# Two attention blocks in one kernel: the first transfers on the sync queue in another order

## The chip, the cores and the metric

The kernel runs on one core of a Trainium2 chip. The metric is the device time of one execution in microseconds (us), as the median of several runs. The core has a matrix engine (TensorE, PE in the rows), a vector engine (VectorE, DVE), an activation engine (ScalarE, ACT), GpSimd (POOL) and a sync engine (SyncE, SP) that in this kernel issues all the transfers. The transfers run on 16 DMA engines behind one queue.

## The reference

The input is `x` and a context, each 64 batches of 128 tokens of width 256 in float32. Block 0 is cross-attention with 16 heads of 64 and an MLP, block 1 is windowed cross-attention with one shared key and value head, a gate and a norm. Cut to what matters:

```python
def block0(q, c):                       # k and v are both the context c
    qn, kn, vn = ln(q, gq, bq), ln(c, gk, bk), ln(c, gv, bv)
    s = einsum(qn Wq, kn Wk) + rel_bias[i - j]
    o = softmax(s / 8) @ (vn Wv) @ fc_w.T + fc_b
    x = q + o
    return x + gelu(ln(x) @ W1.T + b1) @ W2.T + b2

def block1(q, c):                       # one key and value head of 16, window of +-64
    s = where(window, (q Wq + bq)(c Wk + bk) / 4, -1e9)
    a = softmax(s) @ (c Wv + bv) @ Wo + bo
    g = silu([a, q] @ Wg + bg)
    y = a * g + q * (1 - g)
    y = y * rsqrt(mean(y * y) + 1e-6) * rms_w
    return y - mean(y over tokens)
```

## The kernel before

Two batches make a group, and 32 groups are worked through in a software pipeline. Each engine has its own program, a list written out by hand; programs meet only at semaphores (`till.wait_ge(name, count)`), and an engine that waits holds back everything behind it in its list. Float32 weights are split into a high part (ScalarE, `weight_hi_scaled`) and a rest (VectorE, `weight_lo_scaled`), so that a product is three matmuls of a faster type. The gain of the layer norm is multiplied into the weight at that moment, and the shift goes through the weights once, as a matmul (`bias_mm`, one for each half of a weight).

The change lies in the prologue, where the weights, the constants and the data of group 0 come in. The list of transfers stands in `sync_program` (L440 to L457 and on). Weights pass through five staging buffers (`SOFT0`, `SOFTT0`, `HID`, `SOFTT1`, `SOFT1`): half of the query weights goes to SOFT0 and half to SOFTT0, half of the key weights to HID and half to SOFTT1, the first half of the value weights to SOFT1. The second half of the value weights comes later, once more into SOFT0.

Group 0 needs the mean and the reciprocal deviation of each token laid out along the free axis. VectorE takes them from the token-major tiles (`tokens` for x, `first_tokens` for the context; L1477, L1500, L1525, L1533), GpSimd takes the power (L3013, L3021), VectorE transposes (`flip_x` L1543, `flip_c` L1551), and the sync queue writes the result to DRAM (`out_x` L327, `out_c` L354) and reads it back spread over all 128 partitions (`in_x` L331, `in_c` L369). `in_x` waits until what `out_x` wrote has landed, `in_c` the same for `out_c`. The feature-major tiles (`raw_x` L315, `raw_c` L321) are then normalised: x on GpSimd (`x_less` L3051, `x_norm` L3057), the context on VectorE (`first_c_less` L1560, `first_c_norm` L1566). ScalarE makes the high part of x in `x_hi` (L2466).

VectorE's list begins: statistics of x, statistics of the context, `scale_bq1` (L1442, waits for `cols`), `var_c`, `flip_x`. So the flip of x stands behind the context's tokens.
ScalarE's list begins: high parts of the query weights (twice), the key weights (twice), the first half of the value weights, then `x_hi`, `c_hi`, and the second half of the value weights.
TensorE's list begins, in this order:

```python
bias_mm(banks[0], SOFT0, 1, shifts[0], 0)
bias_mm(banks[0], SOFTT0, 1, shifts[0], 1)
bias_mm(banks[2], HID, 1, shifts[1], 0)
bias_mm(banks[2], SOFTT1, 1, shifts[1], 1)
kv(0, banks[0], ("bias", 1))
bias_mm(banks[2], SOFT1, 1, shifts[2], 0, ("bias", 2))
proj_q(0, 0, banks[7])
bias_mm(banks[2], SOFT0, 2, shifts[2], 1)
proj_k(0, 0, banks[1])
```

`cols` holds the gains, shifts and biases that are read by partition (14.5 KB). `relb` holds the relative bias (64 KB), `rows` the constants that are read along the free axis, the same on every partition (648 KB of writes), and `wkv1` the key and value weights of block 1 (32 KB). The last three share the semaphore `consts_in`, which counts to 48. `rows` is first read by `bias_plus` (L1434) and by `kv_out`.

Of the kernel before, what the change touches and what calls it, by code (L numbers as in the profile page):

```python
# [12 lines left out]
P = 128  # L13
# [15 lines left out]

ONCE = ("filled", "ident_made", "masked", "scaled", "bias_mm", "bias_turned", "bias", "w_hi", "w_lo", "bv_hi", "bcol", "fold", "wo_wg",  # L30
        "cols_in", "consts_in", "raw0", "raw1", "raw2", "raw3", "raw4", "x_in", "tokens_in", "raw_in", "stat_out", "stat_in", "stored",
        "keys_out", "keys_in", "spread0", "spread1_0", "spread1_1", "first_tokens", "first_raw", "first_out", "first_in")


def two_block_xattn(nc, t):
# [25 lines left out]
    with ExitStack() as ctx:  # L61
# [27 lines left out]
        rows = sb("rows", [P, 5 * D + HD])  # L89
# [84 lines left out]
        def by_chunk(ap):  # L174
            return ap.rearrange("(k p) n -> p k n", p=P)
# [85 lines left out]
        def sync_program(sp):  # L261
# [115 lines left out]

            def consts_in():
                sp.dma_start(relb[:], t["rel"]).then_inc(sem["consts_in"], 16)
                sp.dma_start(rows[:], t["rows"].partition_broadcast(P)).then_inc(sem["consts_in"], 16)  # L380
                sp.dma_start(wkv1[:], by_chunk(t["wkv1"])).then_inc(sem["consts_in"], 16)

            def q1_gx_in():
                till.wait_ge("w_lo", 11)
# [48 lines left out]
            def store(g, b):  # L433
# [3 lines left out]
                till.wait_ge("y_out", n + 1)  # L437
                sp.dma_start(t["out"][n], gate_of(g, b)).then_inc(sem["stored"], 16)

            tokens_c(0)  # L440
            tokens_x(0)
            weight_in(SOFT0, t["wq_t"][0:P, :])
            cols_in()
            weight_in(SOFTT0, t["wq_t"][P:2 * P, :])
            weight_in(HID, t["wk_t"][0:P, :])
            weight_in(SOFTT1, t["wk_t"][P:2 * P, :])
            consts_in()
            out_x(0)
            raw_x(0)
            out_c(0)  # L450
            weight_in(SOFT1, t["wv_t"][0:P, :])
            raw_c(0)
            in_x(0)
            in_c(0)
            weight_in(HID, half_of(t["fc_t"], 1), ("w_lo", 3), ("bias_mm", 3))
            weight_in(SOFT0, t["wv_t"][P:2 * P, :], ("w_lo", 1), ("bias_mm", 1))
            weight_in(SOFTT0, half_of(t["fc_t"], 0), ("w_lo", 2), ("bias_mm", 2))  # L457
# [149 lines left out]
        def tensor_program(pe):  # L607
# [69 lines left out]
            def kv(g, bank, *drains):  # L677
                if not there(g):
                    return
                if g == 0:  # L680
                    till.wait_ge("consts_in", 48)
                freed(till, *drains)
                src = first_raw if g == 0 else raw[:]
                if g == 0:
                    till.wait_ge("first_raw", 16)
                else:
                    till.wait_ge("raw_in", loads(g, 2))
                for k in range(KD):
                    of_block = src[:, k, :].rearrange("p (b j a) -> p j b a", b=GROUP, j=NB)
                    for j in range(NB):  # L690
                        last = pe.matmul(bank[j * BLOCK:(j + 1) * BLOCK, 0:GROUP * BLOCK], wkv1[:, k, :],
                                         of_block[:, j, :, :], start=(k == 0), stop=(k == KD - 1), skip_group_check=True)
                last.then_inc(sem["kv"], 1)
# [720 lines left out]
        def vector_program(dve):  # L1414
# [15 lines left out]
            def bias_plus(dst, src, stage_of, count):  # L1430
                till.wait_ge(stage_of, count)
                till.wait_ge("cols_in", 16)
                till.wait_ge("consts_in", 48)
                dve.tensor_tensor(dst, src, dst, ALU.add).then_inc(sem["bias"], 1)  # L1434

            def bias_b1(bank):
# [5 lines left out]
                dve.tensor_scalar(bq1[:], bq1[:], -SCALE1, None, ALU.mult).then_inc(sem["scaled"], 1)  # L1442

            def scale_rel():
                till.wait_ge("consts_in", 48)
                dve.tensor_scalar(relb[:], relb[:], -SCALE0, None, ALU.mult).then_inc(sem["scaled"], 1)

            def spread_bv():
# [139 lines left out]
            def kv_out(g):  # L1588
                if not there(g):
                    return  # L1590
                if g == 0:
                    till.wait_ge("consts_in", 48)
                    till.wait_ge("filled", 1)
                till.wait_ge("kv_turn", g + 1)
                if g >= NK1:
# [1915 lines left out]
```

## Time and profile before

| | us |
|---|---|
| median of 3 runs | 1853.11 |
| lowest, highest | 1852.79, 1853.65 |
| the profiled execution's own time | 1853.23 |
| its span in the trace | 1851.4 |
| PE busy in the span | 1798.8 (97%) |
| DVE busy | 1485.9 (80%) |
| ACT busy | 1543.2 (83%) |
| POOL busy | 1294.0 (70%) |

The span is what the trace covers; 1.8 us of the execution lie around it. A row of the time line gives the start, the duration, the engine and line, the operation with the tile it writes and reads, and in brackets how long the engine had been idle and what released it. The row of a transfer on SPq shows only its issue; the time until it has landed is in the view of the DMAs. PE's ends are modelled, so the distance between two starts says more than the duration of one matmul.

### The profile page before, as it was taken

How to read it: one execution, taken by the hardware profiler on the slowest of the kernel's cores; microseconds unless marked ns; L12 is line 12 of the kernel's file. 1: busy time of each engine (PE TensorE's matmuls, PEld its weight loads, DVE VectorE, ACT ScalarE, POOL GpSimd, SP SyncE). 2: the span in 40 equal slices, each digit the busy share in tenths (PEclk: the TensorE clock that was granted, in tenths of full speed). 3: DMA queues.
4: the chain of work that ended last, by engine and by line, in shares of the span. 5: the costliest groups of instructions: out<-in, count | busy, mean ns of one | idle time of the engine just before them, and what ended most of it. 6: DMA issues, size and time to landing. Idle time of an engine off the chain costs nothing.

```text
span 1851.4 us, 54940 instructions
## 1 busy us (share of the span) xinstructions
PE 1798.8 (97%) x18532; PEld 1664.1 (90%) x18532; DVE 1485.9 (80%) x6755; ACT 1543.2 (83%) x5586; POOL 1294.0 (70%) x1324
## 2 busy tenths in 40 slices
PE   6999999999999999999999999999999999999984
PEld 4989999999999999999999999999999999999973
DVE  6878788887788887788887788887888887878764
ACT  4788888888888888888888888888888888888874
POOL 3656777766777766777766777776777776777654
PEclk9999999999999999999999999999999999999997
DMA  7434445444445444444444444444444444444432
GB/s 234 122 97 112 127 116 129 119 110 111 128 117 129 119 112 111 123 121 125 119 114 112 120 125 122 119 119 108 121 123 124 116 119 114 117 116 118 102 87 57
DMA packets 238057, 219.07 MB, mean 118 GB/s; under 512 B 48848, under 2 KB 220240, under 8 KB 237776
## 3 DMA queue, kind: packets, MB, share of 16 engines
q1 hardware_dynamic: 237776, 215.57, 45.4%
q8 instruction: 147, 2.41, 0.5%
q14 instruction: 134, 1.10, 0.2%
HBM read 71.29 MB, written 9.96 MB: 44 GB/s over the span
## 4 chain that ended last, share of the span: by engine, by line
PE 94%; DVE 2%; DMA 1%; POOL 1%; issue 1%; ACT 1%; SPq 0%; POOLq 0%; DVEq 0%
PE bank L611 12%; PE bank L613 11%; PE bank L612 11%; PE bank L625 9%; PE bank L629 8%; PE bank L626 8%; PE bank L779 7%; PE bank L792 7%; PE bank L904 4%; PE bank L917 4%; PE bank L617 3%; PE bank L618 3%; PE bank L621 3%; PE bank L635 2%; DVE soft L1739 1%
## 5 line engine op out<-in xcount | busy, mean ns | idle before, releaser
L2585 ACT ACTIVATE soft<-soft,row_min 128x128 f32<-128x128 f32 x1024 | 397.3, 392 | 65.9 <-DVE row_min L1739 65.8
L2505 ACT ACTIVATE soft<-soft,row_min 128x128 f32<-128x128 f32 x1024 | 398.5, 393 | 17.0 <-DVE row_min L1631 13.1
L3034 POOL TENSOR_TENSOR soft<-soft,inv_sum 128x512 f32<-128x512 f32 x256 | 271.9, 1062 | 169.7 <-DVE inv_sum L1639 169.6
L234 DVE STREAM_TRANSPOSE turned<-soft 128x512 f32<-128x512 f32 x512 | 342.1, 689 | 10.4 <-POOL soft L3034 4.8
L3043 POOL TENSOR_TENSOR soft<-soft,inv_sum 128x512 f32<-128x512 f32 x256 | 264.6, 1045 | 63.5 <-DVE inv_sum L1748 63.4
L1739 DVE CUSTOM_DVE_ANT_0 soft<-bank,winb 128x128 f32<-128x128 f32 x1024 | 230.5, 284 | 44.3 <-PE bank L904 37.2
L1631 DVE CUSTOM_DVE_ANT_0 soft<-bank,relb 128x128 f32<-128x128 f32 x1024 | 230.4, 284 | 22.7 <-PE bank L779 14.0
L2505 ACT ACTIVATION_READ_ACCUMULATOR soft<-soft,row_min 128x1 f32 x1024 | 194.8, 190 | 0.0
L2585 ACT ACTIVATION_READ_ACCUMULATOR soft<-soft,row_min 128x1 f32 x1024 | 194.2, 190 | 0.0
L779 PE MATMUL bank<-kT,qT 64*128 64x128 f32 x2048 | 148.7, 284 | 3.5 <-DVE kT L1611 0.5
L779 PEld LDWEIGHTS bank<-kT,qT 64*128 64x128 f32 x2048 | 125.0, 187 | 26.0 <-issue 20.8
L611 PE MATMUL bank<-wv,cT 128*128 128x256 f32 x512 | 147.6, 288 | 0.0
L613 PE MATMUL bank<-wv,cT 128*128 128x256 f32 x512 | 144.8, 283 | 0.0
L612 PE MATMUL bank<-wv,cT 128*128 128x256 f32 x512 | 144.8, 283 | 0.0
L792 PE MATMUL bank<-soft,V 128*64 128x128 f32 x2048 | 140.1, 279 | 0.7 <-DMA soft<-turned 0.4
L1702 DVE TENSOR_TENSOR hidS<-hid,hidS 128x1024 fp32r<-128x1024 f32 x64 | 84.9, 1326 | 64.4 <-ACT hidS L2556 62.7
L792 PEld LDWEIGHTS bank<-soft,V 128*64 128x64 f32 x2048 | 109.2, 136 | 29.6 <-issue 19.6
L1611 DVE TENSOR_SCALAR kT<-bank,bk 128x256 f32<-128x256 f32 x256 | 110.2, 472 | 29.8 <-PE bank L779 28.2
L625 PE MATMUL bank<-wfc,OT 128*128 128x256 f32 x512 | 133.7, 294 | 0.0
L2487 ACT ACTIVATE qT<-bank,bq 128x256 f32<-128x256 f32 x256 | 106.9, 470 | 31.2 <-PE bank L779 25.5
L626 PE MATMUL bank<-wfc,OT 128*128 128x256 f32 x512 | 127.5, 282 | 0.0
L625 PE MATMUL bank<-w,hidS 128*128 128x256 f32 x512 | 126.9, 281 | 0.0
(247 smaller groups left out, 6495.4 us busy)
## 6 DMA issues: line engine op xcount, KB each, us to landing
soft<-turned SPq DMA_DIRECT2D x1024, 128.0 KB, 2.7
tokens<-stats_by_row SPq DMA_DIRECT2D x63, 256.0 KB, 3.6
tokens<-in_x SPq DMA_DIRECT2D x32, 256.0 KB, 2.7
raw<-in_x_t SPq DMA_DIRECT2D x32, 256.0 KB, 3.3
x<-in_x SPq DMA_DIRECT2D x32, 256.0 KB, 2.7
out<-gate SPq DMA_DIRECT2D x63, 128.0 KB, 2.6
tokens<-in_ctx SPq DMA_DIRECT2D x31, 256.0 KB, 2.8
raw<-in_ctx_t SPq DMA_DIRECT2D x31, 256.0 KB, 2.7
```

The source lines that it names most:

```text
L234: return eng.transpose(turned[:, slot, :, s % 2, :, :].rearrange("p j h b -> p h j b"), soft[:, s, :, :].rearrange("p h (j a) -> p h j a", ...
L611: pe.matmul(out, stat(LO), mov(HI), start=first, stop=False, **kw)
L612: pe.matmul(out, stat(HI), mov(LO), start=False, stop=False, **kw)
L613: return pe.matmul(out, stat(HI), mov(HI), start=False, stop=last, **kw)
L625: pe.matmul(out, stat(HI), mov(LO), start=first, stop=False, skip_group_check=True)
L626: return pe.matmul(out, stat(HI), mov(HI), start=False, stop=False, skip_group_check=True)
L779: last = pe.matmul(bank[i][:, h * SEQ:(h + 1) * SEQ], qT[half, c, b * SEQ:(b + 1) * SEQ], kT[half, c, b * SEQ:(b + 1) * SEQ], start=True, ...
L792: last = pe.matmul(bank[row:row + HS, col:col + SEQ], V[:, b, c * P + row:c * P + row + HS], pair_of_slots(Q % 2)[:, :, slot, h, :], start ...
L2505: last = act.activation(soft[:, s, h, :], soft[:, s, h, :], ACT.Exp, bias=row_min[:, s, h:h + 1], scale=-1.0, accum_out=row_sum[:, s, h:h ...
L2585: last = act.activation(soft[:, s, h, :], soft[:, s, h, :], ACT.Exp, bias=row_min[:, s, h:h + 1], scale=-1.0, accum_out=row_sum[:, s, h:h ...
L3034: pool.tensor_tensor(soft[:, m % NS0, :, :], soft[:, m % NS0, :, :], inv_sum[:, m % NS0, :].unsqueeze(2).broadcast_to([P, QUAD, SEQ]), ALU ...
L3043: pool.tensor_tensor(soft[:, s, :, :], soft[:, s, :, :], inv_sum[:, s, :].unsqueeze(2).broadcast_to([P, QUAD, SEQ]), ALU.mult).then_inc(se ...
```

## The change

The transfers at the head of the sync queue are put in another order. The tokens of x are issued first and the context's tokens fourth; `cols` is issued second instead of fourth. `out_x`, `raw_x` and `in_x` come ahead of the second half of the key weights (`SOFTT1`). Behind that half come `out_c`, the constants, `raw_c` and `in_c`, then the first half of the value weights. The constants lose `rows`, which gets a transfer of its own behind the value weights, and a semaphore of its own (`rows_in`). The waits that counted to 48 now count to 32, or wait for `rows_in` where `rows` is read. The lists of the other engines keep their order.

```diff
             def consts_in():
                 sp.dma_start(relb[:], t["rel"]).then_inc(sem["consts_in"], 16)
-                sp.dma_start(rows[:], t["rows"].partition_broadcast(P)).then_inc(sem["consts_in"], 16)
                 sp.dma_start(wkv1[:], by_chunk(t["wkv1"])).then_inc(sem["consts_in"], 16)
+
+            def rows_of_all():
+                sp.dma_start(rows[:], t["rows"].partition_broadcast(P)).then_inc(sem["rows_in"], 16)
...
+            tokens_x(0)
+            cols_in()
+            weight_in(SOFT0, t["wq_t"][0:P, :])
             tokens_c(0)
-            tokens_x(0)
-            weight_in(SOFT0, t["wq_t"][0:P, :])
-            cols_in()
             weight_in(SOFTT0, t["wq_t"][P:2 * P, :])
             weight_in(HID, t["wk_t"][0:P, :])
-            weight_in(SOFTT1, t["wk_t"][P:2 * P, :])
-            consts_in()
             out_x(0)
             raw_x(0)
+            in_x(0)
+            weight_in(SOFTT1, t["wk_t"][P:2 * P, :])
             out_c(0)
+            consts_in()
+            raw_c(0)
+            in_c(0)
             weight_in(SOFT1, t["wv_t"][0:P, :])
-            raw_c(0)
-            in_x(0)
-            in_c(0)
+            rows_of_all()
             weight_in(HID, half_of(t["fc_t"], 1), ("w_lo", 3), ("bias_mm", 3))
             weight_in(SOFT0, t["wv_t"][P:2 * P, :], ("w_lo", 1), ("bias_mm", 1))
...
                 if g == 0:
-                    till.wait_ge("consts_in", 48)
+                    till.wait_ge("consts_in", 32)
...
             def bias_plus(dst, src, stage_of, count):
...
-                till.wait_ge("consts_in", 48)
+                till.wait_ge("rows_in", 16)
...
             def scale_rel():
-                till.wait_ge("consts_in", 48)
+                till.wait_ge("consts_in", 32)
...
                 if g == 0:
-                    till.wait_ge("consts_in", 48)
+                    till.wait_ge("rows_in", 16)
                     till.wait_ge("filled", 1)
```

## Rows read from the trace of the kernel before

**Rows 1.** The page, part 1: busy time and share of the span.

```profile
PE 1798.8 (97%) x18532; PEld 1664.1 (90%) x18532; DVE 1485.9 (80%) x6755; ACT 1543.2 (83%) x5586; POOL 1294.0 (70%) x1324
```

**Rows 2.** Time line of PE (start, duration, engine, operation, idle before).

```profile
9.41 1.08 PE L645 MATMUL bank<-hid,cols 128*32 128x256 f32 x8
10.71 1.08 PE L645 MATMUL bank<-soft,cols 128*32 128x256 f32 x8 [0.23 <-DMA soft<-in_wk_t]
...
16.78 1.11 PE L645 MATMUL bank<-soft,cols 128*32 128x256 f32 x8
22.13 0.55 PE L617 MATMUL bank<-xT,wq 128*128 128x256 f32 x1 [4.24 <-ACT xT L2466]
...
24.11 1.08 PE L645 MATMUL bank<-soft,cols 128*32 128x256 f32 x8
...
25.50 0.42 PE L618 MATMUL bank<-cT,wk 128*128 128x256 f32 x1
25.72 0.41 PE L617 MATMUL bank<-cT,wk 128*128 128x256 f32 x1
...
27.66 0.28 PE L611 MATMUL bank<-cT,wk 128*128 128x256 f32 x1
27.78 0.28 PE L612 MATMUL bank<-cT,wk 128*128 128x256 f32 x1
```

**Rows 3.** Time line of the sync queue: start and length of an issue.

```profile
0.72 0.45 SPq L301 DMA_DIRECT2D x<-in_ctx  x1
...
7.25 0.69 SPq L327 DMA_DIRECT2D stats_by_row<-stat_rows  x1
...
12.54 0.33 SPq L331 DMA_DIRECT2D tokens<-stats_by_row  x1
13.48 0.32 SPq L369 DMA_DIRECT2D x<-stats_by_row  x1
...
14.33 0.50 SPq L268 DMA_DIRECT2D soft<-in_wv_t  x1
...
33.91 0.52 SPq L327 DMA_DIRECT2D stats_by_row<-stat_rows  x1
35.96 0.33 SPq L331 DMA_DIRECT2D tokens<-stats_by_row  x1
```

**Rows 4.** View of the DMAs, issues at 14.33 and 35.96: KB, us to landing.

```profile
soft<-in_wv_t SPq DMA_DIRECT2D x1, 512.0 KB, 9.4
tokens<-stats_by_row SPq DMA_DIRECT2D x1, 256.0 KB, 3.0
```

**Rows 5.** Windows: engines' busy us (count), then PEclk, DMA share, GB/s.

```profile
5.00:12.00 7.00, 4.32 (x32) 0.81 (x32) 4.43 (x14) 5.25 (x5) 1.42 (x2) 1.00 1.02 388
12.00:15.00 3.00, 0.00 (x0) 0.00 (x0) 2.93 (x6) 0.30 (x1) 0.00 (x0) 1.00 0.90 317
15.20:18.70 3.50, 1.51 (x24) 0.66 (x24) 0.10 (x1) 1.15 (x1) 0.00 (x0) 1.00 0.95 150
18.70:26.20 7.50, 4.07 (x21) 3.07 (x22) 5.19 (x6) 2.38 (x3) 4.23 (x3) 1.00 1.01 358
36.75:38.75 2.00, 2.00 (x26) 1.40 (x23) 1.82 (x11) 1.87 (x5) 1.04 (x1) 1.00 0.38 131
```

**Rows 6.** Time line of DVE: statistics, the wait for cols, first use of rows.

```profile
4.19 0.75 DVE L1477 BATCH_NORM_STATS2 stats<-tokens 128x6 f32<-128x256 f32 x2 [4.19 <-DMA tokens<-in_x]
...
5.34 0.74 DVE L1477 BATCH_NORM_STATS2 stats<-x 128x6 f32<-128x256 f32 x2
...
6.88 0.17 DVE L1442 TENSOR_SCALAR cols<-cols 128x2 f32<-128x2 f32 x1 [0.51 <-DMA cols<-in_cols]
...
50.38 0.42 DVE L1434 TENSOR_TENSOR rows<-bank,rows 128x256 f32<-128x256 f32 x1
```

**Rows 7.** Time line of ACT and POOL: value weights, x's high part, x's statistics.

```profile
6.74 1.28 ACT L2454 ACT_TABLE_LOAD   x1 [6.74 <-DMA soft<-in_wq_t]
...
15.61 1.15 ACT L2454 ACTIVATE wv<-soft,cols 128x1024 fp32r<-128x1024 f32 x1 [3.31 <-DMA soft<-in_wv_t]
21.37 0.62 ACT L2466 CAST xT<-raw 128x512 fp32r<-128x512 f32 x1 [4.61 <-POOL raw L3057]
...
18.73 1.26 POOL L3051 TENSOR_TENSOR raw<-raw,tokens 128x512 f32<-128x512 f32 x1 [10.84 <-DMA tokens<-stats_by_row]
```

More of the change, by code:

```diff
@@ L31 @@
         "cols_in", "consts_in", "raw0", "raw1", "raw2", "raw3", "raw4", "x_in", "tokens_in", "raw_in", "stat_out", "stat_in", "stored",
-        "keys_out", "keys_in", "spread0", "spread1_0", "spread1_1", "first_tokens", "first_raw", "first_out", "first_in")
+        "keys_out", "keys_in", "spread0", "spread1_0", "spread1_1", "first_tokens", "first_raw", "rows_in", "first_out", "first_in")
 def two_block_xattn(nc, t):
```

## The prediction

> **What bounds the kernel now.** I read the shares of busy time first: PE is busy for 1798.8 of the 1851.4 us [rows 1]. The steady part is therefore paced by PE, and work on other engines counts only where PE waits for it. The change touches only the prologue, so the second view is PE's own time line of the first 30 us [rows 2]. After the small bias matmuls of the weights it waits 4.24 us for the high part of x and starts the first projection at 22.13; at 24.11 the bias matmul of the second value weights follows, and from there PE hardly stops. What the change is worth is how much earlier or later PE gets past these two points: the work behind them is fixed.
>
> Next, who holds these points. The x path is a chain of round trips: the flip of x is out at 7.25, what it wrote is seen as landed at 12.54, and what is read back is there at 18.73, when POOL starts [rows 3, 7]. Two POOL operations later ScalarE makes the high part (21.37 [rows 7]) and PE starts 0.76 later [rows 2]. The write and the read are small, but they stand behind weights in the queue: the same pair in group 1, with an empty queue, takes 35.96 - 33.91 = 2.05 and 3.0 us [rows 3, 4], against 5.3 and 6.2 here.
>
> The second point has another holder. The second value weights are issued at 14.33 and land 9.4 us later, at 23.7 [rows 3, 4], 0.4 ahead of PE's bias matmul at 24.11. Between 5 and 26 us the DMA share is 0.90 to 1.02 [rows 5], so nothing but the transfers ahead of it decides this landing. These are the two views to lay side by side: the chain ends in the x path, but the DMA engines are full, and the next thing due is 0.4 us behind it.
>
> **The change part by part.** All times are of the profiled execution.
>
> *Head of the queue.* Ahead of the landing of the context's tokens there are now two token tiles (256 KB each), half of the query weights (512 KB) and cols, which is what stood ahead of the landing of the first weights and cols before: 6.74 and 6.88 [rows 6, 7]. The context's tokens should land at 6.3 to 6.8. I take 6.6. Before, VectorE took them at 5.34 without a wait and then waited 0.51 for cols [rows 6]. The flip of x stands behind them in VectorE's list. From 5.34 to the issue of the write at 7.25 are 1.91 us, less the 0.51: 1.40. So the write of x's statistics is issued at 8.0 (7.7 to 8.2), 0.75 later than before. The first weights land earlier, near 6.0, but the bias matmuls and the weight splits that this starts end in waits for later weights, so it is worth nothing.
>
> *The round trips of x.* Now only the second half of the query weights and the first half of the key weights are ahead of the write; the latter landed at about 9.4 [rows 2]. The write lands at 9.4 at the least and at 8.0 + 2.05 = 10.05 at the most natural; I take 9.9. The read-back is issued then and lands after 3.0 us [rows 4], at 12.9, or 13.4 with raw_x still in front. This is 5.3 us or more ahead of the 18.73 of before. GpSimd then is done with x near 15.6 instead of 21.3. That gain is real, and most of it finds no taker, as follows.
>
> *What now holds PE's first projection.* In PE's list it stands behind the bias matmul of the first value weights, and in ScalarE's list the high part of x stands behind the split of the same weights. Before they landed at 15.6 [rows 7]. Now they stand behind the write and read of both statistics, the second half of the key weights, the small constants and raw_c. The rates of the queue are 512 KB in 1.35 us at 388 GB/s, and a spread read-back of 256 KB in 1.75 us: two of them went through in the 3.5 us from 15.20 at 150 GB/s [rows 5]. The sum: read-back of x starts 0.85 after its issue (the first group's lone read-back moved its bytes from about 36.8 to 38.5 [rows 3, 5]), so 10.75 to 12.5; key weights to 13.8; they land about 1 us behind their last byte, as the key weights and others did. The write of c's statistics lands with them at 14.8, and the read-back of c, which waits for it, is issued at 14.9 and moves from 15.75 to 17.5. The value weights are through at 18.85 and land at 19.7 (19.2 to 20.6). ScalarE then needs 1.15 for the split and 0.62 for the high part [rows 7], and PE starts 0.15 later: 21.6 (21.1 to 22.5) against 22.13. So of 5.3 us there are 0.5 left.
>
> *What holds the second point.* Ahead of the second value weights stand the same bytes as before: nothing was taken out, and rows (648 KB), the second key weights and the rest are all still in front. The queue must be kept full to do it in the same time, and it now runs dry, since the sync engine waits for x's write with nothing behind it issued. The gaps: 8.45 (last byte of the key weights) to 9.55 (raw_x issued 8.7, plus 0.85), 1.1 us; 10.3 to 10.75 before x's read-back, 0.45 us; 14.9 to 15.75 before c's, 0.85 us. Sum 2.4 us. The gaps of before between 12 and 15 are 0.10 of 3 us [rows 5], 0.3 us, and go. Against this, a lone read-back uses only 0.38 of the DMA engines in its 2 us [rows 5], so the weights behind it may flow beside it: a credit between 0 and 1.7 us for two; I take 0.9. Net 2.4 - 0.3 - 0.9 = +1.2 us, from 23.7 to 24.9 (bounds -0.6 with the whole credit and half of the gaps, +3.1 with no credit, larger gaps and c's write landing 1 us late). PE's bias matmul goes from 24.11 to 25.0: **+0.9 us**.
>
> *The clock.* Matmuls of 256 columns start 0.22 apart at 25.5 and 0.12 apart at 27.7 [rows 2]: the 1.2 GHz and the 2.4 GHz level, though the column of the granted clock shows 1.00 in all these stretches [rows 5]. The rise came at 26.3, after 4.2 us without a pause. The busy but broken stretch of bias matmuls from 6.9 to 11.8 brought none: the one at 10.71 takes 1.08 us for its eight, as the one at 24.11 does [rows 2]. With a pause from 23.5 (the end of the first projection) to 25.0, the rise may come 4.2 us after 25.0 instead of 2.2 after 24.11. Two more us at half speed cost 2.0 x (1 - 0.12 / 0.22) = 0.9. If the pause does no harm, the rise comes earlier relative to the work and returns up to 0.6. I take **+0.6**.
>
> *Moved waits.* The relative bias and wkv1 are waited for by the first kv matmul on PE and by scale_rel on VectorE; both stand behind or beside weights that land at 14.8 or later, and cost nothing. rows lands near 21.5 now and is first read at 50.38 [rows 6]: nothing, with 29 us of cover.
>
> *Sum:* 0.9 + 0.6 = +1.5 us. The profiled execution took 1853.23 and the median is 1853.11, so 1854.7 on either to within 0.1.
>
> A rule of the Trainium skill speaks against the change: "SBUF — State Buffer", section "The DMA setup-cost knee", says that every DMA pays about 2 us that don't depend on its size, mostly until its completion is confirmed. By that rule two round trips that nothing covers would put 4 us or more of empty queue ahead of the value weights, an estimate of 1857 or above. The trace agrees on the size (2.05 us for the 16 KB write [rows 3]); but in part other transfers are in flight meanwhile, which is why my gaps come to 2.4 us and not to 4.
>
> **The rivals.**
> A, *the DMA engines catch up*. The weights flow beside both read-backs (for it: the share of 0.38; against it: 0.95 when both were queued between weights, at 150 GB/s [rows 5]). The second value weights land at 23.3 or before, the first projection starts at 21.3 and is followed without a pause: -0.8 us, 1852.3. With everything in its favour, the first projection at 20.3: -1.8 us, 1851.3. It cannot be more, as the bytes alone need until about 22.
> B, *slower: the blocked sync engine*. The read-back of c waits for c's write, which lands only with the key weights in front of it. If landing lags by 2 us, as the second value weights do behind the bytes, the value weights are pushed by 2.7 us; with the late clock (0.9), and 0.4 for the later weights of fc, it comes to +4.0: 1857.1. It decides from a landing of the second value weights at 26.5 on.
> C, *nothing moves*. The landing stays within 0.4 us of 23.7, PE's list is the same, 1853.1.
> D, *gain by more than 3.7 us*. The x path would have to be the only holder, with PE starting 4 us earlier and never stopping for the value weights. The full DMA share speaks against it; 1848.5.
>
> **How the numbers follow.** My forecast (+0.5 to +3, 1853.6 to 1856.2) has 0.45; A 0.22; C 0.13; B 0.13; D 0.07. The range must reach from A's far end to B: 1850.9 to 1857.6, which leaves out D and the far end of B, some 0.15. A change of 0.2% (3.7 us) is about what a measurement of this kernel can tell from none: faster than 1849.4 is D with a little of A, 0.08; slower than 1856.8 is most of B, 0.12; between them 0.80.
>
> **What would show it.** Right: the write of x's statistics issued near 8.0, x's read-back landed near 13, POOL starting there; the first value weights landing at 19 to 20.5, later than before; a hole in the DMA share between 8.5 and 11 and before c's read-back; the bias matmul at L645 waiting for the second value weights near 25. Wrong: if PE starts the first projection before 20, if the DMA share has no hole, if the second value weights land before 23.5, or if the time differs while PE's start doesn't, since then the difference arises in the steady part, which I hold to be fixed.

## The result and the profile after

The changed kernel takes 1857.34 us in the median of 14 runs, the kernel before 1854.43 in 14 runs on the same chips: a ratio of 1.0017 with a 95% interval of 1.0009 to 1.0024, that is +3.1 us (1.7 to 4.5). The three runs of before that the prediction started from lie at the lower end of these 14 (1852.42 to 1856.2). The span of the profiled execution grew from 1851.4 to 1854.7.

PE is busy for the same time as in [rows 1]. Page of the changed kernel, part 1:

```profile
PE 1798.2 (97%) x18532; PEld 1663.7 (90%) x18532; DVE 1485.5 (80%) x6755; ACT 1543.1 (83%) x5586; POOL 1294.2 (70%) x1324
```

So the page puts the 3.3 us down to time in which PE isn't busy, and doesn't say where it lies. That is read best from a mark that each kernel passes 64 times, the stores of the output. Issues on the sync queue of before, then of the changed kernel (start, length): the first store, one near 1741 us and the last.

```profile
155.52 0.43 SPq L438 DMA_DIRECT2D out<-gate  x1
...
1741.53 0.34 SPq L438 DMA_DIRECT2D out<-gate  x1
...
1849.28 0.34 SPq L438 DMA_DIRECT2D out<-raw  x1
```

```profile
159.40 0.43 SPq L440 DMA_DIRECT2D out<-gate  x1
...
1745.40 0.34 SPq L440 DMA_DIRECT2D out<-gate  x1
...
1852.56 0.34 SPq L440 DMA_DIRECT2D out<-raw  x1
```

The delay is 3.9 us at the first store and 3.9 at 1741: all of it arises before 155 us and none is added or recovered in the steady part. The last groups return 0.6. (In the runs below the last groups move by up to 1.3 us either way between executions, so I compare by the delay at the stores, or "store shift", and by the ratio.)

Now the time line of PE, which answers to [rows 2]; lines are three higher than before:

```profile
9.77 1.08 PE L648 MATMUL bank<-hid,cols 128*32 128x256 f32 x8
16.51 1.08 PE L648 MATMUL bank<-soft,cols 128*32 128x256 f32 x8 [5.66 <-DMA soft<-in_wk_t]
...
21.54 1.08 PE L648 MATMUL bank<-soft,cols 128*32 128x256 f32 x8 [3.37 <-DMA soft<-in_wv_t]
23.23 0.55 PE L620 MATMUL bank<-xT,wq 128*128 128x256 f32 x1 [0.61 <-ACT xT L2469]
...
26.66 1.08 PE L648 MATMUL bank<-soft,cols 128*32 128x256 f32 x8 [1.38 <-DMA soft<-in_wv_t]
...
29.54 1.05 PE L624 MATMUL bank<-cT,wk 128*128 128x256 f32 x4
30.39 1.05 PE L624 MATMUL bank<-xT,wq 128*128 128x256 f32 x4
31.25 0.37 PE L614 MATMUL bank<-cT,wk 128*128 128x256 f32 x1
31.45 0.28 PE L615 MATMUL bank<-cT,wk 128*128 128x256 f32 x1
31.57 0.28 PE L616 MATMUL bank<-cT,wk 128*128 128x256 f32 x1
...
34.29 1.16 PE L782 MATMUL bank<-kT,qT 64*128 64x128 f32 x16
```

Before, PE's long wait was the one for the high part of x (4.24 [rows 2]); now it waits 3.37 for the first value weights, only 0.61 for the high part of x, and 1.38 for the second value weights. The first projection starts at 23.23 instead of 22.13, the bias matmul of the second value weights at 26.66 instead of 24.11 (+2.55), and the first scores at 34.29. Before, these scores started at 30.63:

```profile
30.63 1.16 PE L779 MATMUL bank<-kT,qT 64*128 64x128 f32 x16
```

That is +3.66, of which 2.55 is the bias matmul and 1.11 came in behind it (the way from the bias matmul to the scores takes 7.63 instead of 6.52). In that stretch starts of 256 columns are 0.21 apart (1.2 GHz) up to 31.3 and 0.12 apart (2.4 GHz) from then on; before, the change of level was at 26.3.

The two chains behind it. Sync queue, answering to [rows 3]:

```profile
8.71 0.69 SPq L327 DMA_DIRECT2D stats_by_row<-stat_rows  x1
9.45 0.42 SPq L315 DMA_DIRECT2D raw<-in_x_t  x1
10.83 0.33 SPq L331 DMA_DIRECT2D tokens<-stats_by_row  x1
...
15.85 0.33 SPq L369 DMA_DIRECT2D x<-stats_by_row  x1
16.22 0.44 SPq L268 DMA_DIRECT2D soft<-in_wv_t  x1
```

Windows, answering to [rows 5] (busy us of PE, PEld, DVE, ACT, POOL, then PEclk, DMA share, GB/s). The kernel before in the same stretches, then the changed one:

```profile
8.50:13.50 5.00, 2.93 (x24) 0.40 (x16) 4.25 (x7) 3.80 (x4) 0.00 (x0) 1.00 0.98 356
13.50:16.00 2.50, 0.00 (x0) 0.00 (x0) 1.76 (x4) 0.39 (x1) 0.00 (x0) 1.00 0.96 293
16.00:18.70 2.70, 1.51 (x24) 0.66 (x24) 0.00 (x0) 0.76 (x1) 0.00 (x0) 1.00 0.95 141
```

```profile
8.50:13.50 5.00, 2.16 (x16) 0.40 (x16) 4.47 (x8) 2.66 (x3) 0.70 (x1) 1.00 0.44 127
13.50:16.00 2.50, 0.00 (x0) 0.00 (x0) 0.00 (x0) 0.00 (x0) 0.66 (x1) 1.00 0.98 327
16.00:18.70 2.70, 1.66 (x24) 0.64 (x24) 1.01 (x3) 1.15 (x1) 1.88 (x2) 1.00 0.49 138
18.70:26.20 7.50, 3.12 (x16) 2.01 (x16) 5.23 (x6) 2.18 (x3) 1.90 (x1) 1.00 1.01 361
```

The share of the DMA engines falls from 0.98 to 0.44 while the sync engine waits for x's statistics, and from 0.95 to 0.49 around the context's. Multiplied out, (1 - share) x length is 2.8 + 1.4 = 4.2 us against 0.1 + 0.1 before. I call this the dry time. The second value weights land at 17.65 + 9.0 = 26.6 instead of 23.7.

The dry time overstates the loss, since the share says how long the engines were taken and not what they moved: in the stretch from 16.0 to 18.7 it is 0.95 against 0.49, yet both kernels move the same there (141 and 138 GB/s). In bytes, the three rows from 8.5 to 18.7 (GB/s times us) add up to 2893 KB before and 1825 KB after. The missing 1068 KB take 3.0 us at the 360 GB/s of the stretch behind it, and the landing moved by 2.9. (Up to 8.5 the changed kernel is another 0.14 MB behind, 0.4 us, so this holds to about half a us.) The shift of the landing isn't an accident of one execution either: the transfers of the changed kernel were traced three times (here, e4 and e8 below), with landings at 26.6, 26.3 and 27.3, those of the kernel before twice (the second is e12), at 23.7 and 23.8.

x's statistics themselves are early, as the change meant them to be. Time line of POOL, answering to [rows 7]:

```profile
15.34 1.26 POOL L3054 TENSOR_TENSOR raw<-raw,tokens 128x512 f32<-128x512 f32 x1 [6.00 <-DMA tokens<-stats_by_row]
16.68 1.28 POOL L3060 TENSOR_TENSOR raw<-raw,tokens 128x512 f32<-128x512 f32 x1
23.16 1.90 POOL L3092 TENSOR_TENSOR xT<-raw,xT 128x512 fp32r<-128x512 f32 x1 [5.20 <-ACT xT L2469]
```

POOL has x normalised at 18.0 instead of 21.3 and then waits 5.20 us for the high part, which stands behind the value weights in ScalarE's list. The gain of 3.4 us is there and nobody takes it.

### The profile page after: what moved, and what is told of

Read it like the earlier page. It is cut to its first block, busy times and chain, and to the rows that moved or that the text cites. A ratio compares the mean times of both kernels' runs of the same rounds, so it can differ in the third digit from the quotient of the medians.

```text
span 1854.7 us, 54941 instructions
## 1 busy us (share of the span) xinstructions
PE 1798.2 (97%) x18532; PEld 1663.7 (90%) x18532; DVE 1485.5 (80%) x6755; ACT 1543.1 (83%) x5586; POOL 1294.2 (70%) x1324
## 4 chain that ended last, share of the span: by engine, by line
PE 94%; DVE 2%; DMA 1%; issue 1%; POOL 1%; ACT 1%; SPq 0%; POOLq 0%; DVEq 0%
PE bank L614 12%; PE bank L615 11%; PE bank L616 11%; PE bank L628 9%; PE bank L632 8%; PE bank L629 8%; PE bank L782 7%; PE bank L795 7%; PE bank L907 4%; PE bank L920 3%; PE bank L620 3%; PE bank L624 3%; PE bank L621 3%; PE bank L638 2%; DVE soft L1742 1%
## 5 line engine op out<-in xcount | busy, mean ns | idle before, releaser
L1634 DVE CUSTOM_DVE_ANT_0 soft<-bank,relb 128x128 f32<-128x128 f32 x1024 | 230.3, 283 | 22.8 <-PE bank L782 14.0
L1614 DVE TENSOR_SCALAR kT<-bank,bk 128x256 f32<-128x256 f32 x256 | 110.1, 471 | 29.8 <-PE bank L782 28.2
```

## The experiments

The theory has two parts. **Dry time:** the sync engine's waits let the queue run dry, and what is lost there comes back as a later landing of the second value weights. **The level:** the new pause keeps PE at its low level (1.2 GHz) for longer behind that landing. The rivals: the landing follows from which bytes stand where; the landing alone costs and the level doesn't; or x's statistics are what counts.

The table gives, from each trace, when the second value weights land (landing), where PE starts their bias matmul (bias) and the first scores, the store shift against before, and the ratio of the times with its interval. One caution: kernels with the same head of the queue start their first bias matmul between 5.9 and 7.0 us from one execution to the next, and e3, with the same bytes in front as the kernel before, has its second value weights 1.5 us earlier. So a single trace is good to 0.5 to 1 us, and a ratio to some 1.6 us. Most of the runs below therefore speak by their traces, one each; the intervals of the ratios tell few of them apart.

| kernel | landing | bias | scores | store shift | ratio |
|---|---|---|---|---|---|
| before | 23.7 | 24.11 | 30.63 | 0 | 1 |
| changed | 26.6 | 26.66 | 34.29 | +3.9 | 1.0017 [1.0009, 1.0024] |
| e1, key weights first | 24.2 | 24.24 | 32.49 | +2.1 | 1.0012 [1.0004, 1.0021] |
| e2, rows alone | 24.2 | 24.27 | 31.23 | +1.1 | 1.0005 [0.9997, 1.0014] |
| e3, head alone | 22.2 | 22.85 | 29.42 | -0.6 | 0.9998 [0.9989, 1.0006] |
| e4, changed, busy (128 columns) | 26.3 | 31.77 | 37.32 | +7.4 | 1.0042 [1.0030, 1.0054] |
| e5, rows last | 22.8 | 23.80 | 30.83 | +0.4 | 1.0001 [0.9992, 1.0010] |
| e6, and value weights ahead | 20.8 | 23.06 | 30.06 | 0.0 | 0.9994 [0.9985, 1.0002] |
| e8, changed, busy (256 columns) | 27.3 | 27.38 | 32.94 | +3.0 | 1.0009 [1.0001, 1.0018] |
| e9, queue kept full | 20.7 | 20.80 | 28.26 | -2.0 | 0.9989 [0.9980, 0.9998] |
| e10, e9 and busy | 21.5 | 21.49 | 27.46 | -2.5 | 0.9984 [0.9975, 0.9993] |
| e11, changed, values ahead of the context's read-back | 24.7 | 24.82 | 32.21 | +1.8 | 1.0016 [1.0007, 1.0025] |
| e12, before, busy | 23.8 | 23.86 | 32.07 | +1.6 | 0.9998 [0.9990, 1.0007] |
| e13, e10 with both value weights ahead | 19.7 | 20.87 | 31.98 | +1.5 | 1.0004 [0.9995, 1.0013] |

**e1: the second key weights back in front**

```diff
             weight_in(HID, t["wk_t"][0:P, :])
+            weight_in(SOFTT1, t["wk_t"][P:2 * P, :])
             out_x(0)
             raw_x(0)
             in_x(0)
-            weight_in(SOFTT1, t["wk_t"][P:2 * P, :])
```

> The changed kernel with one line back: the second half of the key weights is issued ahead of the write of x's statistics again, so that the DMA engines have 512 KB more to do while the sync engine waits. Theory (the queue runs dry during the two waits, and each dry us is a us on the landing of the second value weights): the hole after 8.7 us shrinks by about 1.3 us, these weights land at 25.0 to 25.4 instead of 26.6, PE's bias matmul follows, and the time is 1.3 to 2 us under the changed kernel's, +1.3 to +2 us against before (ratio 1.0007 to 1.0011). Rival (the loss comes from the later place of the small transfers and of the context's write, not from dry time): the landing stays at 26.6 and the ratio at 1.0017.

The bias matmul starts at 24.24, 2.4 us earlier than in the changed kernel. Windows of e1, the same stretches:

```profile
8.50:13.50 5.00, 2.60 (x23) 0.40 (x16) 4.93 (x9) 2.99 (x3) 0.11 (x1) 1.00 0.72 224
13.50:16.00 2.50, 0.66 (x16) 0.45 (x16) 0.99 (x1) 0.00 (x0) 2.22 (x2) 1.00 0.61 184
16.00:18.70 2.70, 0.00 (x0) 0.00 (x0) 0.64 (x2) 0.00 (x0) 0.95 (x1) 1.00 0.92 336
```

By the same multiplication 2.6 us are dry instead of 4.2. So one 512 KB transfer in front of the wait fills 1.6 us, about what its bytes need. The other 0.7 us are luck: the first weights landed that much earlier in this execution (first bias matmul at 5.99 instead of 6.70). The weights landed at 24.2, 2.4 earlier, where I had expected 25.0 to 25.4. The rival, that the bytes' order costs and not the dry time, expected no move of the landing and falls. But the shift is still +2.1 although the bias matmul is back to within 0.1 of before: PE stayed at its low level until 30.4, and the way from the bias matmul to the scores took 8.25 us instead of 6.52. That is more than the pause of the changed kernel cost, with a shorter pause in front (0.97 against 1.38). The ratio, 1.0012, lies just above what I had expected, and its interval holds both that and the rival's 1.0017.

**e2: rows alone moved** (order of before otherwise; rows behind `in_c(0)`, own semaphore)

> The kernel before with one part of the change alone: rows (648 KB) has its own semaphore and is issued behind the read-back of the context's statistics instead of behind the key weights. It is still ahead of the second value weights. Theory (the bytes ahead of the second value weights decide): x's read-back lands some 1.6 us earlier (17.0 instead of 18.7), the first projection starts up to 1.6 us earlier, but the second value weights land at 23.7 as before and PE's bias matmul at 24.1 does not move: 0 us, within 0.4, ratio 0.9998 to 1.0002. Rival (the x path alone holds PE): -1.6 us, ratio 0.9991.

The bias matmul did not move (24.27 against 24.11; the weights landed at 24.2 against 23.7), though x's read-back was there at 17.47 instead of 18.73 and PE began the first projection at 20.87. The rival that x's path alone holds PE falls: its ratio, 0.9991, is outside the interval. The store shift is +1.1 and not 0: 0.44 of it came in on the way to the scores, where PE was longer at its low level behind a pause of 1.35 us, and 0.5 behind the scores. The measured ratio can't tell it from 1.

**e3: the head alone** (kernel before with `tokens_x, cols_in`, first query weights, `tokens_c`)

> The kernel before with only the first four transfers in the changed order (tokens of x, cols, first query weights, tokens of the context). Theory: the write of x's statistics is issued at 8.7 instead of 7.25, as in the changed kernel, since the flip stands behind the context's tokens; but the queue is filled to beyond 11 us, so the write lands at 12.5 as before and nothing moves: 0 us, ratio 0.9998 to 1.0003. Rival (the late flip itself costs): +1.4 us, ratio 1.0008.

The write of x's statistics was issued at 8.70, 1.45 us later than before, and nothing was lost: 0.9998. The interval leaves out the rival's 1.0008: the late flip costs nothing here, where the queue has work. In this trace the bias matmul was even 1.26 us earlier, which the ratio doesn't confirm.

**e11: the second wait**

```diff
             raw_c(0)
+            weight_in(SOFT1, t["wv_t"][0:P, :])
             in_c(0)
-            weight_in(SOFT1, t["wv_t"][0:P, :])
```

> The changed kernel with the first value weights issued ahead of the read-back of the context's statistics (the second wait of the sync engine), so that 512 KB more are in the queue while it waits for the context's write. Theory: the hole near 16 to 17 us shrinks by some 0.7 us, the first value weights land 2 to 2.5 us earlier and with them the first projection, the second value weights land 0.7 us earlier (26.0): with the clock, 0.7 to 1.2 us under the changed kernel, ratio 1.0010 to 1.0013. Rival (only the first hole, at 9 to 11 us, costs): 1.0017.

```profile
8.50:13.50 5.00, 1.62 (x16) 0.20 (x8) 4.14 (x6) 1.89 (x2) 0.11 (x1) 1.00 0.56 152
...
16.00:18.70 2.70, 2.11 (x32) 0.67 (x24) 1.81 (x3) 1.61 (x2) 1.12 (x1) 1.00 0.95 307
```

The second hole is closed (share 0.95 instead of 0.49, and 307 instead of 138 GB/s), and the bias matmul starts at 24.82, 1.8 us before the changed kernel's; the first one's 0.8 us of head start in this execution is part of that. The ratio, 1.0016, shows no gain that could be told from the changed kernel's; its trace has a store shift of 1.8 and then loses 1.3 in the last groups. So the trace speaks for the second hole and the times leave it open.

**e4 and e8: the level.** Matmuls that nobody reads in PE's waits of the changed kernel. In e4 they multiplied 128 columns:

```diff
+            def keep_busy(n):
+                till.wait_ge("filled", 1)
+                for _ in range(n):
+                    pe.matmul(banks[5][:, 0:P], center[:], center[:], start=True, stop=True)
...
             kv(0, banks[0], ("bias", 1))
+            keep_busy(32)
             bias_mm(banks[2], SOFT1, 1, shifts[2], 0, ("bias", 2))
+            keep_busy(5)
             proj_q(0, 0, banks[7])
+            keep_busy(18)
```

> The changed kernel with matmuls that nobody reads (128 columns, into a bank that is free then): 32 behind the first kv, 5 ahead of the first projection, 18 between it and the bias matmul of the second value weights. Theory of the clock (a pause in PE's work delays the rise to the higher level, 31.2 us instead of 26.3): the rise comes before 24, the bias matmul still waits for the weights at 26.6, and the 4.6 us of work behind it that ran at the low level take 2.6: about -2 us against the changed kernel, ratio to before 1.0006. Rival (the late rise costs nothing, only the landing counts): no difference to the changed kernel, ratio 1.0017.

That experiment failed by its own price (1.0042 where I had expected 1.0006): 128 columns took as long as 256 do. Time line of PE of e4:

```profile
18.25 7.09 PE L964 MATMUL bank<-center 128*128 128x128 f32 x32
25.27 1.08 PE L648 MATMUL bank<-soft,cols 128*32 128x256 f32 x8
...
29.22 2.62 PE L964 MATMUL bank<-center 128*128 128x128 f32 x18
31.77 0.64 PE L648 MATMUL bank<-soft,cols 128*32 128x256 f32 x8
```

32 of them held PE for 7.09 us, 0.22 each, and put the real work off by 5 us. Yet it shows something: PE had no pause from 18.25 on and was still at the low level at 29.0 (0.21 us from start to start in the projection). Once the bias matmul ran at the high level (0.64 for its eight instead of 1.08), the way to the scores took 5.55 us. e8 repeats it with the projection's own shape and fewer of them:

```diff
+            def keep_busy(n):
+                till.wait_ge("w_lo", 2)
+                for _ in range(n):
+                    pe.matmul(banks[5][:, 0:2 * P], wq[:, HI, 0, 0:P], wq[:, HI, 0, 0:2 * P], start=True, stop=True)
...
             kv(0, banks[0], ("bias", 1))
+            keep_busy(15)
             bias_mm(banks[2], SOFT1, 1, shifts[2], 0, ("bias", 2))
+            keep_busy(2)
             proj_q(0, 0, banks[7])
+            keep_busy(6)
```

> The changed kernel with matmuls that nobody reads, this time of the same shape and operands' kind as the projection's (256 columns, 0.21 us each at the low level): 15 behind the first kv, 2 ahead of the first projection, 6 between it and the bias matmul of the second value weights. Nothing waits longer for PE if they take that time. Theory of the clock (the pauses at 18 to 21.5 and at 25.3 to 26.7 delay the rise; at the low level each us of work behind costs 0.44 us): the rise comes before the bias matmul at 26.6 instead of at 31.3, the scores start 2 us earlier than in the changed kernel; time 1.5 to 2 us under it, ratio to before 1.0006 to 1.0009. Rival (only the landing counts): as the changed kernel, 1.0017.

```profile
18.39 3.57 PE L964 MATMUL bank<-wq 128*128 128x256 f32 x15
22.34 0.64 PE L648 MATMUL bank<-soft,cols 128*32 128x256 f32 x8 [0.38 <-DMA soft<-in_wv_t]
...
27.38 0.64 PE L648 MATMUL bank<-soft,cols 128*32 128x256 f32 x8 [1.50 <-DMA soft<-in_wv_t]
```

The level is high from about 22 on and holds over the pause of 1.50. The landing is not earlier (27.38; this execution's head was 0.3 late), but from there to the scores it is 5.56 us instead of 7.63: 2.1 us earlier by the work alone. The store shift is 3.0 against 3.9 and the ratio 1.0009 against 1.0017. The point values agree with the theory and not with the rival, but the interval of e8 (1.0001 to 1.0018) holds the rival's 1.0017. So the trace shows that the level is worth 2.1 us here; the times don't confirm it.

**e5, e6: rows last, value weights ahead**

> The kernel before with rows (648 KB, own semaphore) moved behind all of the prologue's weights, so that it is no longer ahead of the second value weights. It is first read near 50 us. Theory (the bytes ahead of the second value weights decide when PE passes its bias matmul): they land 1.6 us earlier, near 22.1, x's read-back too, PE starts the first projection near 20.9 and passes the bias matmul at 22.9 instead of 24.1 without a pause: -1.2 us, ratio 0.9993. Rival (nothing in the first transfers matters within the noise): ratio 1.0000.

> As the run with rows last, and the second value weights one place further ahead of the 512 KB of fc weights. Theory: their landing comes another 1.3 us earlier, but PE is then held by x's read-back, which is not moved: the same as with rows last, -1.2 us, ratio 0.9993. If it is 1.3 us better, x's read-back was not the holder.

The trace of e5 missed in an instructive way. With 648 KB less in front, x's read-back was issued at 12.47 and was there at 18.4, almost as before (12.54 and 18.73). The second value weights landed 0.9 earlier, but the first projection started only at 21.82 and the bias matmul behind it at 23.80, without a wait for the weights. Windows of e5:

```profile
8.50:10.70 2.20, 1.90 (x19) 0.41 (x16) 1.31 (x2) 2.20 (x3) 0.00 (x0) 1.00 1.04 370
10.70:12.70 2.00, 1.36 (x12) 0.20 (x8) 1.97 (x5) 1.78 (x2) 0.00 (x0) 1.00 0.27 89
12.70:18.70 6.00, 1.51 (x24) 0.66 (x24) 2.74 (x4) 1.15 (x1) 0.27 (x1) 1.00 0.82 225
```

Where rows had been moved, the queue ran dry (share 0.27): the sync engine was waiting until 10.8 for the context's flip, which is set by VectorE. rows in its old place was the cover of that wait. The kernel before has the same wait. This is the view of what its sync engine waited for in the first 20 us (us in total, times, longest):

```profile
SPq L354 <- DVE first_rows L1551: 2.2, 1, 2.2
...
SPq L189 <- DMA stats_by_row<-stat_rows: 0.3, 1, 0.3
```

So what put off x's read-back to 12.54 was not the landing of x's write (0.3 us of waiting) but the wait for the context's flip in front of it in the list. Bytes taken from in front of a wait give little if the next transfer can't be issued sooner. The ratio of e5, 1.0001, is not told apart from my 0.9993 nor from the rival's 1.0000. e6 came out at 0.9994 with its bias matmul at 23.06, both close to what I had expected, but its store shift is 0.0: not told apart from before either.

**e9: early statistics and a full queue**

```diff
             weight_in(HID, t["wk_t"][0:P, :])
+            weight_in(SOFTT1, t["wk_t"][P:2 * P, :])
             out_x(0)
             raw_x(0)
+            weight_in(SOFT1, t["wv_t"][0:P, :])
             in_x(0)
-            weight_in(SOFTT1, t["wk_t"][P:2 * P, :])
             out_c(0)
             consts_in()
             raw_c(0)
             in_c(0)
-            weight_in(SOFT1, t["wv_t"][0:P, :])
-            rows_of_all()
+            weight_in(SOFT0, t["wv_t"][P:2 * P, :], ("w_lo", 1), ("bias_mm", 1))
             weight_in(HID, half_of(t["fc_t"], 1), ("w_lo", 3), ("bias_mm", 3))
-            weight_in(SOFT0, t["wv_t"][P:2 * P, :], ("w_lo", 1), ("bias_mm", 1))
...
             weight_in(SOFT1, t["w1_t"][P:2 * P, :], ("w_lo", 5), ("bias_mm", 5))
+            rows_of_all()
```

> An order in which the changed kernel's early statistics are kept and the queue does not run dry: both halves of the key weights ahead of the write of x's statistics, raw_x and the first value weights between that write and the read-back, then the context's write, the small constants, raw_c and its read-back, then the second value weights ahead of the fc weights, rows last. Theory (dry time and bytes ahead decide): the second value weights land near 19 to 20, the first projection starts near 18, PE passes the bias matmul near 20 instead of 24.1: -3.5 to -4.6 us against before, ratio 0.9975 to 0.9981. Rival (a fixed steady part absorbs an earlier start, since another engine then holds it): above 0.999.

```profile
8.50:13.50 5.00, 2.79 (x24) 0.41 (x16) 4.93 (x9) 3.47 (x4) 0.15 (x1) 1.00 0.96 327
13.50:18.70 5.20, 2.42 (x28) 1.60 (x29) 1.00 (x1) 1.42 (x2) 3.51 (x3) 0.64 0.64 172
```

The first hole is gone (0.96), the second is not (0.64). In this stretch the column of the granted clock shows 0.64 too: it is 0.50 from about 15 to 25 us, which is where the starts are 0.21 apart. It does so as well in e12 (from 23) and in e13 (from 20); in all other traces it stays at 1.00 while the same spacing shows the low level, so in this prologue the spacing is the safer reading. The first projection starts at 17.78 and the bias matmul at 20.80, 3.3 us before the kernel before, and the ratio is 0.9989: under the kernel before, by less than I expected (0.9975 to 0.9981). 0.9 us of the 3.3 are lost on the way to the scores, which takes 7.46 instead of 6.52, and another 0.4 between the scores and the first store. The rival, a steady part that absorbs an earlier start, had said above 0.999; the interval, 0.9980 to 0.9998, reaches into both.

**e10, e12, e13: the level where the queue is full, in the kernel before, and with a longer pause.** All with `keep_busy` of e8. e10 is e9 with 19 ahead of the first kv and 5 behind the first projection; e12 is the kernel before with 18 ahead of the first kv and 18 ahead of the first projection; e13 is e9 with 19 ahead of the first kv and the second value weights issued ahead of `in_c(0)`.

> The order that kept the queue full (it passed the bias matmul of the second value weights at 20.8 and the scores started at 28.3, with PE at its low level until 25.7), with unread matmuls of the projection's shape in PE's waits: 19 ahead of the first kv, 5 behind the first projection. Theory of the clock: PE is at the high level before 20.8, the way from the bias matmul to the scores takes 5.6 us (as in the changed kernel with such matmuls) instead of 7.5, the scores start near 26.4, and the time is 1.5 to 2 us under that order's: ratio to before 0.9978 to 0.9982. Rival: no further gain, 0.9989.

> The kernel before, its transfers untouched, with unread matmuls of the projection's shape in PE's waits: 18 ahead of the first kv, 18 between the bias matmul of the first value weights and the first projection. Theory of the clock: PE is at the high level before 22.1, the 2.2 us of work at the low level behind the bias matmul cost no more; the scores start 1.0 to 1.3 us earlier: ratio 0.9993 to 0.9995. Rival: 1.0000.

> The order that kept the queue full, with the second value weights also ahead of the read-back of the context's statistics (what is left of that wait is covered), and 19 unread matmuls ahead of the first kv. Theory (dry time): the second value weights land before 19, PE goes from the first projection to the bias matmul without a pause near 19, and is then held by the context's high part, near 20.5 to 21: another 0 to 0.8 us, ratio 0.9974 to 0.9980. Rival (the context's read-back behind 512 KB more becomes the holder): slower than the order without it.

e10 takes 1851.05 in the median against 1853.96, ratio 0.9984 [0.9975, 0.9993]: below both kernels, and less than the 0.9978 to 0.9982 that I had expected, though the interval holds them. From the bias matmul to the scores it needs 5.97 instead of 7.46 us. Against e9 (0.9989) the difference is within the intervals.

e12 went the wrong way in its trace:

```profile
16.99 2.42 PE L961 MATMUL bank<-wq 128*128 128x256 f32 x18
21.53 0.38 PE L617 MATMUL bank<-xT,wq 128*128 128x256 f32 x1 [2.12 <-ACT xT L2473]
...
23.86 1.08 PE L645 MATMUL bank<-soft,cols 128*32 128x256 f32 x8 [1.12 <-DMA soft<-in_wv_t]
```

The high level was reached, so the 18 took 2.42 us and not the 3.8 I had laid out; PE then waited 2.12 us, did the projection at the high level (1 us), waited 1.12 more, and the bias matmul ran at the low one again. It stayed low until 29.8, the scores came at 32.07 (+1.4). The times show no loss (0.9998), so other executions probably fell differently; that isn't shown. e13 is the same with a longer wait: the second value weights landed early (bias matmul at 20.87), but the context's read-back stood behind them, PE waited 2.59 us for the context's high part (24.54), at the low level from 20.1 to 30.0, and all of the gain of e9 was gone. The rival written for it held.

**Putting the traces together.** With L the time from the bias matmul to the rise of the level, each of these us is worth 1 - 0.12/0.213 = 0.44. The way to the scores is then 5.56 (e8, all high) + 0.44 L: before, L = 2.2, 6.5 (measured 6.52); changed, L = 4.7, 7.6 (7.63); e1, L = 6.2, 8.3 (8.25); e9, L = 4.4, 7.5 (7.46); e12, L = 6.0, 8.2 (8.21). Five traces agree to 0.1 us, so up to the scores the change's 3.66 is 2.55 of the bias matmul and 1.11 of level, and nothing else. Between the scores and the first store each trace has another 0.2 to 0.7 us against the kernel before (the changed one 0.2), which I did not trace.

What the sum doesn't show is that the pause made L longer. Where PE went from the first projection to the bias matmul without a pause, the way took 6.52 (before), 6.57 (e3), 7.03 (e5) and 7.00 us (e6); behind a pause of 1.0 to 3.1 us it took 6.96 (e2), 7.39 (e11), 7.46 (e9), 7.63 (changed) and 8.25 (e1). The second group is slower in the mean, by 0.8 us, but they overlap, and the longest way stands behind the shortest pause but one. So some 0.5 us of the 1.11 may be a difference between executions. The price of a late rise is shown; that the pause causes it is likely and not shown for the changed kernel alone.

## Why the prediction was right, point by point

The forecast of +1.5 us with a range of -2.2 to +4.5 (1850.9 to 1857.6 against 1853.11) held the measured +3.1; the sign was right, and the size is at double the forecast. The result is outside the forecast's own case (+0.5 to +3.0, given 0.45) and nearer to rival B (+4.0, given 0.13). As a time, 1857.34 is only 0.3 us inside the range, partly because the kernel before came out at 1854.43 in its 14 runs. So the chain of causes was right, and the width of the range carried the size.

- *PE is the bound and only its start counts*: right up to 1741 us: the delay is 3.9 there and at the first store. The last groups add or return up to 1.3 us, which the prediction had as fixed.
- *Head of the queue*: the context's tokens landed at 7.3, not 6.6, and the write was issued at 8.71 instead of 8.0. e3 shows that this by itself costs nothing; here, with nothing queued behind, it opens the hole by 0.7 us more.
- *The 5.3 us of x's write in the kernel before*: misread. I put them down to weights in front of the write; by the view of the sync engine's waits (under e5) the wait for the context's flip held the list, and the write itself only 0.3 us. It did no harm to the sum, which takes the write at its lone 2.05.
- *x's round trips*: the read-back was there at 15.34, not 13. It was issued at 10.83 (I had 9.9) and took 4.4 us and not 3.0 [rows 4], with raw_x in front of it. Still earlier than PE could use it, so the miss cost nothing by itself.
- *What holds the first projection*: right in kind, the value weights through ScalarE's list, but out of its bounds: they landed at 21.4 and not at 19.2 to 20.6, and the projection started at 23.23 (forecast 21.6). Where I saw 0.5 us left of the gain, 1.1 us were lost.
- *What holds the second point*: the term that was mis-sized. I had 2.4 us of gaps less 0.3 and a credit of 0.9 for weights flowing beside the read-backs, +1.2 in all. The bytes not moved make 3.0 us, and the landing moved by 2.9 (the bias matmul by 2.55). The credit was wrong: in the stretch from 16.0 to 18.7, with the context's read-back in it and the value weights queued behind, the changed kernel moved 138 GB/s with 0.49 of the engines' time taken, where the kernel before moved 141 at 0.95. The weights did not fill the rest, so the share of 0.38 [rows 5] was room that nobody used. Without the credit the sum is +2.1; the write of x's statistics, issued 0.7 later than forecast, brings it to 2.8.
- *The clock*: a late rise came and cost 1.1 (+0.6 forecast, 0.9 with the pause at its worst). e1 and e8 show its price in their traces, one with the bias matmul restored and the level not, one the other way round. The forecast built on a rise 4.2 us after the last pause, which did not hold: from the bias matmul it took 4.7 in the changed kernel, 6.2 in e1, 4.4 in e9 and 3.3 in e2. How near the size came is in part luck.
- *Moved waits*: right; no row shows a wait for rows or the constants.
- *The rule on the fixed cost of a DMA*: its estimate of 4 us or more came nearer to the measured +3.1 than my sum of +1.5. By that rule ("SBUF — State Buffer" of the Trainium skill, "The DMA setup-cost knee") every DMA pays about 2 us that don't depend on its size. The trace agrees for x's write, issued at 8.71, with the read-back that waits for it at 10.83. That both round trips count in full it doesn't bear out: the bytes not moved make 3.0 us, as part of the second wait was covered (share 0.98 from 13.5 to 16.0). And of the +3.1 a part is the level, which the rule knows nothing of.
- *Rival A* (a catch-up) is out; its premise was the credit. *Rival B* came within 0.9 us. Its point of decision was a landing at 26.5, and it landed at 26.6, so by that sign the case is B's, at its lower edge. Its mechanism is in the trace too: the context's read-back, waiting for the context's write, was issued at 15.85 and not at 14.9.

## What to carry to other kernels

In a prologue that is bound by its transfers, look at the share of the DMA engines before the chain of waits: if it is full, a round trip brought forward is paid for by whatever is not issued while the queue's engine waits. Put a wait only where enough bytes have been issued in front of it to cover it, and before taking a big transfer away ask which wait it was covering (e5). And where TensorE starts late, count the level as well as the landing: with the bias matmul at the same place, the scores came 1.7 us later at the low level (e1 against before, one trace each).

## What the runs showed that I had not expected

- When the level rises and falls I could not have said beforehand. In e4 PE had no pause from 18.25 to 29.2, the first 7 us of it with matmuls of 128 columns, and was still at 1.2 GHz. In e8, with matmuls of 256 columns from 18.39 on, it was at 2.4 GHz at 22.34. In e12 it had fallen after waits of 2.12 and 1.12 us with a projection between them; in e8 it held over one of 1.50. Why, no run here shows.
- At the low level a matmul of this type with 128 columns took as long as one of 256 (0.22 us in e4 against 0.21).
- While the statistics were read back, 2 KB of DRAM onto each of the 128 partitions, the DMA engines moved some 140 GB/s: 141 before with two read-backs queued, 138 in the changed kernel with one and weights behind it.
- Between executions of the same head, the first weights land up to 1.1 us apart (5.93 in e11, 7.03 in e8), which is a third of what the whole change moves.
